# A bias inside a matrix product: one wide product for the bank, or one row product before each tile

## The reference

```python
# layer 0, its end: y is the filtered neighbour sum after its activation
y = jnp.einsum('bid,ed->bie', y, Wd2) + bd2
# layer 1, between the attention sum and the map back
support_t = jax.nn.silu(t @ mlp_w1.T + mlp_b1) @ mlp_w2.T + mlp_b2 + x_self
```

## Time and profile before

| | |
|---|---|
| three runs | 2708.28, 2708.28 and 2710.97 us; median 2708.28 |
| profiled execution, its own time | 2708.28 us |
| its span, first to last instruction | 2706.5 us |
| mean granted TensorE clock | 0.954 of 2.4 GHz |
| TensorE busy | 2389.4 us (88%) |
| VectorE busy | 2226.4 us (82%) |
| ScalarE busy | 2066.1 us (76%) |
| POOL busy | 1773.4 us (66%) |

### The profile page before, as it was taken

The page is one execution under the profiler, slowest core; times in us unless marked ns, Lnnn a source line. Parts: engine busy times, 40 slices in busy tenths (PEclk is TensorE's granted clock), DMA queues, the critical chain, the costliest instruction groups (busy, mean ns, idle before and its releaser), DMA issues. The chain is left out here.

```text
span 2706.5 us, 63062 instructions
## 1 busy us (share of the span) xinstructions
PE 2389.4 (88%) x25296; PEld 1171.3 (43%) x25296; DVE 2226.4 (82%) x3819; ACT 2066.1 (76%) x1938; POOL 1773.4 (66%) x1149
## 2 busy tenths in 40 slices
PE   4899999999999999999996388879898989898863
PEld 2333333333333333333332244546565656555543
DVE  6699898998989989899897864788888888885556
ACT  5888888888888888888883267777777777776741
POOL 0699888998989989889893254545454545454421
PEclk8899999999999999999998689989899989999996
DMA  8899998998999999999870446655565656566520
GB/s 235 172 198 202 195 200 194 199 200 194 202 193 200 196 196 202 195 199 202 192 170 26 93 109 108 133 99 136 104 135 104 135 106 127 104 123 114 86 61 20
DMA packets 312067, 410.27 MB, mean 152 GB/s; under 512 B 91488, under 2 KB 284640, under 8 KB 286688
## 3 DMA queue, kind: packets, MB, share of 16 engines
q1 hardware_dynamic: 311776, 406.23, 71.3%
HBM read 368.38 MB, written 35.65 MB: 149 GB/s over the span
## 5 line engine op out<-in xcount | busy, mean ns | idle before, releaser
L684 POOL TENSOR_TENSOR f_gate<-rfT,f_sq 128x1024 f32<-128x1024 f32 x512 | 1219.3, 2382 | 225.1 <-DVE f_prod L699 147.2
L617 PE MATMUL PS<-f_h,w_W2T 64*64 64x512 f32 x8192 | 997.9, 591 | 10.0 <-PE PS L617 1.8
L699 DVE SCALAR_TENSOR_TENSOR f_prod<-PS,b2l,f_gate 128x1024 f32<-128x1024 f32 x512 | 657.3, 1284 | 145.4 <-PE PS L617 109.5
L1195 ACT ACTIVATE a_silu<-PS,c_att_b 128x1024 f32<-128x1024 f32 x512 | 544.6, 1110 | 202.7 <-PE PS L1023 200.4
L579 ACT ACTIVATE f_h<-PS,c_b 128x1024 f32<-128x1024 f32 x512 | 556.3, 1112 | 165.4 <-PE PS L599 164.7
L691 DVE TENSOR_REDUCE yT<-f_prod 128x16 f32<-128x1024 f32 x512 | 618.6, 1208 | 0.0
L1337 POOL TENSOR_TENSOR a_outer<-a_by_i,a_by_j 128x256 f32<-128x256 f32 x512 | 358.8, 726 | 354.3 <-PE PS L1023 340.7
L617 PEld LDWEIGHTS PS<-f_h,w_W2T 64*64 64x64 f32 x8192 | 340.5, 133 | 561.1 <-issue 437.7
L599 PE MATMUL PS<-f_gauss,W1two 64*64 64x512 f32 x4096 | 545.2, 594 | 7.1 <-ACT f_gauss L566 4.8
L1023 PE MATMUL PS<-a_outer,a_rows 32*128 32x128 f32 x8192 | 392.9, 296 | 123.9 <-ACT a_silu L1195 82.2
L1023 PEld LDWEIGHTS PS<-a_outer,a_rows 32*128 32x128 f32 x8192 | 316.8, 194 | 336.0 <-issue 140.6
(11 more groups left out here) (244 smaller groups left out, 2142.2 us busy)
## 6 DMA issues: line engine op xcount, KB each, us to landing
f_gauss<-in_adj SPq DMA_DIRECT2D x128, 1024.0 KB, 11.7
f_sq<-adj_sq SPq DMA_DIRECT2D x256, 512.0 KB, 8.8
a_rows<-hw_d SPq DMA_DIRECT2D x1024, 64.0 KB
hw_d<-b_xc SPq DMA_DIRECT2D x16, 512.0 KB, 4.7
hw_d<-b_sq SPq DMA_DIRECT2D x16, 512.0 KB, 6.4
b_x<-in_x SPq DMA_DIRECT2D x8, 512.0 KB, 3.9
x_d<-b_x SPq DMA_DIRECT2D x8, 512.0 KB, 6.3
h_d<-b_h SPq DMA_DIRECT2D x8, 512.0 KB, 6.0
```

What stands on the lines that cost most here:

```text
L617: PE.matmul(post("message", c)[rows[b], n, :], W2T[rows[k], rows[fh]], hidden(c, n)[rows[k], b, :], start=not second, stop=bool(second)).t ...
L684: GP.tensor_tensor(by_pair(GATE[c % GATE_BUFS][:]), rf, by_pair(squares), ALU.mult).then_inc(s_gate, 1)
L699: V.scalar_tensor_tensor(PR[c % PR_BUFS][:], post("message", c).rearrange("p b n -> p (b n)"), b2l[:, c % 2:c % 2 + 1], GATE[c % GATE_BUFS ...
L1195: A.activation(SI[p % SI_BUFS][:], PS[:, first:first + 2, :].rearrange("p b n -> p (b n)"), ACT.Silu, bias=cols["att_b1"][:]).then_inc(s_s ...
```

## The change

The bias of a fill is no longer one product over the bank. Before each of the four data products there is now one with a contraction of one row: weights are the first row of `ones` (1 by 128), the moving operand is the first row of the bias (1 by 128), into the same 128 columns. It starts the sum of its 128 columns, and the data product adds to it and closes it. The empty `SHIFT` and its use are taken out as well.

```diff
-SHIFT = {}
...
-        live += [Paced(chains[c](slot + ahead), slot * TICKS + SHIFT.get((c, slot + ahead), 0)) for c, ahead in AHEAD.items() if 0 <= slot + ahead < GROUPS]
+        live += [Paced(chains[c](slot + ahead), slot * TICKS) for c, ahead in AHEAD.items() if 0 <= slot + ahead < GROUPS]
...
         def per_tile_and_bias(n, lhs, rhs, bias, h):
             free(n)
-            PE.matmul(bank(n), ident[:, 0:1].broadcast_to([P, P]), bias[:].unsqueeze(1).broadcast_to([P, HALF_GT, P]),
-                      start=True, stop=True)
             for k in range(HALF_GT):
-                last = PE.matmul(bank(n)[:, k, :], lhs(h * HALF_GT + k), rhs, start=False, stop=True,
-                                 skip_group_check=True)
+                PE.matmul(bank(n)[:, k, :], ones[0:1, :], bias[0:1, :], start=True, stop=False)
+                last = PE.matmul(bank(n)[:, k, :], lhs(h * HALF_GT + k), rhs, start=False, stop=True)
             last.then_inc(s_fill, 1)
```

## The result

The changed kernel takes 2779.74 us (median of 4 runs, 2771.51 to 2786.45) against 2709.62 us, 70 us more; over all runs of both it is 1.025 times as long, 95% interval 1.0231 to 1.0268, some 68 us. The forecast was 2741 us, with a range up to 2758. The direction was right; the loss is twice the size.

A forecast was written before the change was run, and what follows sets the result against it. The prediction took the chain of waits through TensorE's program as the bound, TensorE and VectorE being level and neither full. Path terms 20.8 + 4.1 + 2.7 + 3.1 + 2.4 = 33 us on 2708.3 gave 2741 us, range 2722 to 2758.

The forecast's parts named there:

- The mechanism and its price: In each last-stage fill: every change of array shape exposes a weight load, 0.19 us; new fill 3.1 or 3.3 us.
- The rule that changing the mode drains the engine: At bias/data switches on TensorE: a skill rule without a price, taken to agree with 0.19 us a switch.
- absorbed: Rival: longer fills mostly replace TensorE's 11.2 us a slot waiting for silu; half or less of 33 arrives, 2714 to 2728; chance 0.10.
- the sum over the path at full clock: Last-stage fills on the path: four slots 20.8, slot at 2121 4.1, z0/z1 at 2523 2.7, tail 3.1, head 2.4; 33 us.
- all of it, and the clock: Rival: hidden fills surface too, 43 us, 2751; a clock fall in seven slots adds 14, up to 2765; chance 0.12.
- The head: First group's y0 and y1 at the stage's start: 1.35 + 1.55 less 0.5 free, so 2.4 us on the path.
- The cover that was taken for 2.7 us at 2402: z0, z1 at 2402: their extra 2.7 us hidden before waits of 0.94 and 1.65 us for rows from memory.
- The cover at 1596: y0, y1 at 1596: their extra 2.5 us hidden, as the slot then waits 3.36 us for rows from memory.
- The rule on weight loads: Second passes in fills: loads overlap only across row groups, 0.9 us a fill, some 20 us more; left out of the sum.

The follow-up runs named there:

- z0 and z1 alone: Two kernels, each with the new fill form in only z0 or only z1, other three fills as before: 8 us and 12 us over the kernel before.
- the whole-array run: Changed kernel, but each of the four in-turn bias products uses all 128 rows of weights: 1.0013 times the kernel before, 3.5 us more.
- the dots put between: Changed kernel with z1 one tick later, so a dot product stands between z0 and z1: 1.0202 times the kernel before, 55 us more; its control 0.9999.
- 32 rows are slightly cheaper than one: Changed kernel with 32 rows of weights in each bias product in place of one: 1.0212 times the kernel before, 57 us more.
- the lead alone: Kernel before with the new fill form in y0 and y1 only, z0 and z1 keeping the wide bias product: 1.0097 times the kernel before, 26 us more.

## Why the prediction was wrong

**The mechanism and its price were right.** A product of one row is a tile of its own, each change to and from the whole array leaves a weight load that nothing hides, and a change costs 0.19 to 0.2 us: a fill at full clock takes 3.12 us after the inputs and 3.33 otherwise, against 3.1 and 3.3. z0 and z1 alone cost 8 and 12 us, near their direct terms of 9.6 and 12.4. The rule that changing the mode drains the engine (the Trainium skill, TensorEngine Tiling (Array Packing), Key Properties) holds here, with the runs' price of 0.2 us; the whole-array run shows that nothing else in the change has a direct price. The changes between one row and 32 rows are free. The rival "absorbed" is out: TensorE's waits for silu are 82.2 us before and 82.6 after. (Half or less of 33 us would have ended it at 2725 us, not at 2728.)

**The step that failed is the sum over the path at full clock: 20.8 + 4.1 + 2.7 + 3.1 + 2.4 = 33 us.** It priced each fill by rows taken at full clock and left the granted clock as it was; the clock stood only in the rival "all of it, and the clock", with a chance of 0.12, 2 us of work a slot and a ceiling of 2765 us. Measured, it is as large as the direct cost: z1 takes 3.6 to 5.7 us in place of 3.3 in all its fills, the two to four products behind it 0.3 to 0.9 us more each, and 65 us more of the slots pass at 1.2 GHz, 54 of them in and behind the pairs z0, z1 and 14 in and behind single y fills. That the pair of z matters as a pair is shown by its parts (20 us apart, 41 together) and, more weakly, by the dots put between (13 us less). The prediction did work out that the columns stream only half the time in 6.6 us, and priced the fall that might follow at 2 us of work a slot. It gives no reason for holding it unlikely; beside it stand the granted clocks of 0.97 and 0.74 and that TensorE is busy less than half in the tail. Busy time was the wrong thing to look at: TensorE was busy throughout.

**The head** was a term of 2.4 us, with y0 and y1 at full clock as they ran before. They run at half clock from the first pass, the add comes 8 us later and the attention starts 8.6 us later. Keeping the old form there starts the attention 7 us earlier and gives some 6 us back.

**The cover that was taken for 2.7 us at 2402** gave way: that slot got 5.5 us longer. The waits for rows there, 0.94 and 1.65 us, are gone in the changed kernel's trace; they could hide the direct 2.7 us but not z1 at half clock (5.37 us in the profiled run) and the four products behind it, 3 us more together. The cover at 1596, 3.36 us, held: -0.3 us.

**The rule on weight loads.** By the Trainium skill (TensorE: Matmul & The Clock Gate, Part 3) a weight load overlaps only a product of another row group; the prediction's estimate from it was 20 us more, a time near 2761. The runs at full clock contradict the rule: in the whole-array run, as in the kernel before, each pass starts 0.11 us after the last in the same row group, and in the changed kernel the second pass of each two ends 0.11 us after the first.

**What stays open.** Why the clock falls in some single fills and not in others, and at another place in each z1, isn't shown. Slots with the same fills differ by more than 4 us (7.0 to 11.5). And 32 rows are slightly cheaper than one.

## What to carry to other kernels

Before putting a small product between large ones, look at the shape that the profile gives each of them: a change of shape cost 0.2 us each way here, and grouping the small ones first brings eight changes down to one or two (8 us in place of 68). When a change thins out TensorE's work without leaving it idle, price the clock as well: a busy share of 100% says nothing, the granted clock of the stretch and the length of the same pass before and behind it do. And give each shifted kernel its control, since a product may be covering another engine's wait.

## What the runs showed of the hardware

The granted clock fell from 1.00 to 0.51 with TensorE busy for all of 4.00 and 6.30 us by the profile, where each second pass brought a change of shape. It did so in all eight pairs of such fills back to back, in one of eight when z0 or z1 alone was such a fill (z1 alone: 7 of 8 fills at 3.33 us), and in four of 12 single y fills in the slots, in the changed kernel and with the lead alone. In the slots of the kernel before and of the whole-array run it never fell without a wait of TensorE ahead of it. A product with one row of weights has the shape 1*128 and goes behind 32*128 without a stop: the fill takes 3.12 us there, 0.21 less than behind any other shape.
